# Attention with a stabilised softmax: row maxima moved by half batches of 16 heads, scores 19 fills ahead of the weights instead of 28

## What is computed

```python
q = (Q @ w_q.T).reshape(B, S, G, HG, HD)      # 8 groups of 4 heads, width 8; B = 4, S = 256
k = (K @ w_k.T).reshape(B, S, G, HD)
v = (V @ w_v.T).reshape(B, S, G, HD)
scores = jnp.einsum('bnghd,bmgd->bnghm', q, k) / scale
scores = jnp.where(pad, NEG_INF, scores)
scores = jnp.where(causal, scores, NEG_INF)
attn = jax.nn.softmax(scores, axis=-1)
out = jnp.einsum('bnghm,bmgd->bnghd', attn, v).reshape(B, S, D)
return out @ w_o.T + b_o
```

## Time and profile before

| | before |
|---|---|
| time, median of 3 runs | 359.84 us |
| profiled execution: time | 358.81 us |
| profiled execution: span | 357.1 us |
| busy: TensorE matmul / VectorE / ScalarE / POOL | 318.0 / 258.3 / 162.8 / 110.3 us |
| granted TensorE clock, mean over the span | 0.976 |
| first score, first weight, first matmul of the FFN | 139.60 / 163.76 / 275.10 us |
| granted clock from 150 to 320 us | 1.00 |

### The profile page before, as it was taken

The page is one execution under the profiler, slowest core; times in us unless marked ns, Lnnn a source line. Parts: engine busy times, 40 slices in busy tenths (PEclk is TensorE's granted clock), DMA queues, the critical chain, the costliest instruction groups (busy, mean ns, idle before and its releaser), DMA issues.

```text
span 357.1 us, 5054 instructions
## 1 busy us (share of the span) xinstructions
PE 318.0 (89%) x1630; PEld 218.0 (61%) x1639; DVE 258.3 (72%) x572; ACT 162.8 (46%) x333; POOL 110.3 (31%) x156
## 2 busy tenths in 40 slices
PE   2799886669999987999989999998979999999997
PEld 1385676547899634555544554563444886788885
DVE  4538895776677649989967996895672479999921
ACT  2333455344444222147767766775784344333000
POOL 7503575272000275501443425243554001000000
PEclk9999999658999999999999999999999999999999
DMA  6999200025311224600000000000000000000101
GB/s 190 369 418 323 51 1 16 2 88 180 101 61 59 76 59 130 284 0 9 0 7 2 1 0 9 0 3 1 6 3 0 0 2 0 2 0 0 46 30 44
DMA packets 14090, 22.96 MB, mean 64 GB/s; under 512 B 2065, under 2 KB 11409, under 8 KB 13202
## 3 DMA queue, kind: packets, MB, share of 16 engines
q1 hardware_dynamic: 13298, 20.56, 16.8%
q0 software_dynamic: 768, 2.10, 1.9%
HBM read 16.36 MB, written 6.03 MB: 63 GB/s over the span
## 4 chain that ended last, share of the span: by engine, by line
PE 61%; DVE 21%; issue 5%; ACT 4%; DMA 4%; POOL 4%; SPq 1%; DVEq 0%; ACTq 0%; POOLq 0%
PE bank L272 44%; DVE mx L1332 6%; PE bank L492 5%; PE bank L460 4%; ACT region L1008 3%; DVE stats L1078 2%; PE bank L463 2%; DMA region<-y_sorted,place 2%; PE bank L288 2%; POOL rstd L774 2%; DVE x_sb L1118 1%; DVE xn L1090 1%; PE bank L282 1%; PE bank L507 1%; POOL region L814 1%
## 5 line engine op out<-in xcount | busy, mean ns | idle before, releaser
L1008 ACT ACTIVATE region<-bank,padcol 128x512 f32<-128x512 f32 x96 | 62.3, 692 | 18.6 <-PE bank L272 17.8
L1332 DVE TENSOR_REDUCE mx<-bank 128x2 f32<-128x512 f32 (+1 forms) x96 | 60.9, 681 | 4.7 <-PE bank L463 4.1
L841 POOL TENSOR_SCALAR_AFFINE_SELECT region<-region 128x1024 f32<-128x1024 f32 x32 | 35.8, 1121 | 77.8 <-ACT region L1008 77.8
L272 PE MATMUL bank<-qst,kblk 128*128 128x512 f32 x96 | 45.7, 488 | 0.8 <-DMA qst<-nmT 0.3
L460 PE MATMUL bank<-kblk,qst 128*128 128x512 f32 x96 | 43.6, 471 | 1.7 <-DVE mx L1332 1.3
L463 PE MATMUL bank<-causb,identb 128*128 128x256 bf16 (+1 forms) x90 | 28.3, 314 | 0.0
L272 PE MATMUL bank<-e_down,region 128*128 128x256 f32 x128 | 28.0, 380 | 0.0
L1118 DVE SCALAR_TENSOR_TENSOR x_sb<-bank,tg,x_sb 128x256 f32<-128x256 f32 x24 | 11.6, 483 | 21.0 <-PE bank L272 21.0
L272 PEld LDWEIGHTS bank<-e_down,region 128*128 128x128 f32 x128 | 24.2, 190 | 3.6 <-DVE region L1481 0.3
L774 POOL TENSOR_TENSOR rstd<-veps,power 128x1 f32<-128x1 f32 x40 | 24.8, 619 | 3.3
L770 POOL TENSOR_SCALAR veps<-mv 128x1 f32<-128x1 f32 x40 | 12.8, 321 | 40.3 <-DVE mv L1080 37.5
(11 more groups left out here) (195 smaller groups left out, 737.0 us busy)
## 6 DMA issues: line engine op xcount, KB each, us to landing
e_gu<-in_e_gu_dram SPq DMA_DIRECT2D x2, 1408.0 KB, 12.2
x_sorted<-zero SPq DMA_DIRECT2D x1, 1920.0 KB, 9.4
y_sorted<-region SPq DMA_DIRECT2D x15, 128.0 KB, 1.7
x_sb<-in_x_dram SPq DMA_DIRECT2D x4, 256.0 KB, 4.1
ctxT<-in_ctxT_dram SPq DMA_DIRECT2D x2, 512.0 KB, 7.3
e_down<-in_e_down_dram SPq DMA_DIRECT2D x1, 1024.0 KB, 13.6
region<-x_sorted SPq DMA_DIRECT2D x1, 1024.0 KB, 7.4
e_gu<-in_f_gate_dram SPq DMA_DIRECT2D x1, 1024.0 KB, 6.5
```

What stands on the lines that cost most here:

```text
L272: return pe.matmul(dst, lhsT, rhs, start=first, stop=last)
L841: pool.affine_select(out=block, in_=block, compare_op=ALU.is_ge, fill=0.0, base=0, pattern=[[0, 2], [0, PER_GROUP], [1, P]], channel_multi ...
L1008: taken(act.activation(dst, src.rearrange("p (h n) -> p h n", n=SEQ - mt * P), ACT.Exp, bias=padcol[:, key:key + 1], scale=float(HD) ** -0 ...
L1332: taken(dve.reduce_max(mx[:, b % 2, nt, quads, q, hg], src, AX), "sa")
```

## The change

The maxima travel in halves of 16 heads: `negate`, `neg_turn` and the pair of transfers are done per half, after score fills 11 and 23, each with half of the columns; the second half's weights (fill 12) have a wait of their own. `nmx` and `nmT` have a slot per half instead of one per batch parity. Both transposes of a half go into one bank, with one wait and one copy. So scores need to be only 12 fills plus `LEAD` = 7 ahead of the weights, 19, where they ran 24 + 4 = 28 ahead (31 at the beginning). In the steps of a batch scores stand at steps 0 to 16; seven score fills of the next batch stand at the end of each, three before and four behind the last value product.

```diff
-LEAD = 4
-FIRST_LEAD = 7
+HALF_FILLS = 12
+LEAD = 7
-NEGATE_AT, FIRST_NEGATE_AT = 22, 18
+NEGATE_AT, FIRST_NEGATE_AT = (7, 19), 13
...
-            def neg_turn(b, kinds):
-                s = b % 2
+            def neg_turn(b, q):
+
+                half = 2 * b + q
+                dst = acquire(pe, "nmT", half, "turn1")
+                pe.wait_ge(sem("nm_made"), 2 * half + 2)
                 for nt in range(2):
-                    dst = acquire(pe, "nmT", 2 * b + nt, kinds[nt])
-                    pe.wait_ge(sem("nm_made"), 2 * b + nt + 1)
-                    ready(pe.transpose(dst[0:2 * HEADS, 0:P], nmx[:, s, nt, :].bitcast(F32), ident[:, :]), "nmT")
+                    ins = pe.transpose(dst[0:HEADS, tile_cols(nt)], nmx[:, q, nt, :].bitcast(F32), ident[:, :])
+                ready(ins, "nmT")
...
-                if n == 0:
-                    pe.wait_ge(sem("max_rows"), 16 * 2 * (b + 1))
+                if n % HALF_FILLS == 0:
+                    pe.wait_ge(sem("max_rows"), 16 * 2 * (2 * b + q + 1))
...
-            for n in range(24):
+            for n in range(HALF_FILLS + LEAD):
                 scores(0, n)
                 if n in (1, 3):
                     stack_piece(0, 2 + n // 2, "exp")
+                if n == FIRST_NEGATE_AT:
+                    neg_turn(0, 0)
                 queries(1, n)
-                if n >= 20:
-                    stack_piece(1, n - 20, "exp")
-            for n in range(FIRST_LEAD):
-                scores(1, n)
-                if n == 2:
-                    neg_turn(0, ("turn1", "tok1"))
+                if n >= HALF_FILLS + LEAD - 2:
+                    for piece in range(2):
+                        stack_piece(1, 2 * (n - HALF_FILLS - LEAD + 2) + piece, "exp")
             for b in range(BATCH):
-                lead = LEAD if b else FIRST_LEAD
                 for n in range(24):
-                    if b + 1 < BATCH and n + lead < 24:
-                        scores(b + 1, n + lead)
+                    ahead = 24 * b + n + HALF_FILLS + LEAD
+                    if n + LEAD < 24 and ahead < 24 * BATCH:
+                        scores(*divmod(ahead, 24))
                     weights(b, n)
...
-                    if n == (NEGATE_AT if b else FIRST_NEGATE_AT) and b + 1 < BATCH:
-                        neg_turn(b + 1, ("turn1", "turn1"))
+                    if n == NEGATE_AT[0]:
+                        neg_turn(b, 1)
+                    if n == NEGATE_AT[1] and b + 1 < BATCH:
+                        neg_turn(b + 1, 0)
...
                     for n in range(i * LEAD // 2, (i + 1) * LEAD // 2):
-                        if b + 2 < BATCH:
-                            scores(b + 2, n)
+                        if b + 1 < BATCH:
+                            scores(b + 1, HALF_FILLS + n)
...
-            for b in range(BATCH):
-                sp.wait_ge(sem("nmT_taken"), 2 * b + 2)
+            for half in range(BATCH * HALVES):
+                b, q = divmod(half, HALVES)
+                sp.wait_ge(sem("nmT_taken"), half + 1)
...
+            def row_maxima_at(at):
+
+                b, n = divmod(at, 24)
+                row_maxima(b, n)
+                if n % HALF_FILLS == HALF_FILLS - 1:
+                    negate(b, n // HALF_FILLS)
...
             for b in range(BATCH):
-                lead = LEAD if b else FIRST_LEAD
-                if b + 1 < BATCH:
-                    for n in range(lead):
-                        row_maxima(b + 1, n)
+                if b >= 1:
+                    for n in range(LEAD):
+                        row_maxima_at(24 * b + HALF_FILLS + n)
                 for n in range(24):
-                    if b + 1 < BATCH and n + lead < 24:
-                        row_maxima(b + 1, n + lead)
-                        if n + lead == 23:
-                            negate(b + 1)
+                    ahead = 24 * b + n + HALF_FILLS + LEAD
+                    if n + LEAD < 24 and ahead < 24 * BATCH:
+                        row_maxima_at(ahead)
```

More of the change, by code:

```diff
@@ L743, in _ @@
             load(sp, "f", f_down, a["f_down"])
-            for b in range(BATCH):
-                sp.wait_ge(sem("nmT_taken"), 2 * b + 2)
+            for half in range(BATCH * HALVES):
+                b, q = divmod(half, HALVES)
+                sp.wait_ge(sem("nmT_taken"), half + 1)
+                if half >= 1:
+                    sp.wait_ge(sem("max_rows"), 16 * 2 * half)
                 for piece in range(2):
-                    rows = slice(piece * HEADS, (piece + 1) * HEADS)
-                    dst = qst[24 + piece:P:32, b % 2, :, :, :]
-                    sp.dma_start(dst.rearrange("p q h n -> p (q h) n").bitcast(F32),
-                                 nmT[rows, b % 2, :].bitcast(F32))\
+                    rows = slice(piece * HEADS // 2, (piece + 1) * HEADS // 2)
+                    sp.dma_start(qst[24 + piece:P:32, b % 2, q, :, :].bitcast(F32), nmT[rows, q, :].bitcast(F32))\
                       .then_inc(sem("max_rows"), 16)
@@ L989, in _, with neg_turn @@
                 act.activation(s_high[0:EXPERT_R, 2 + i % 2, 1, :], src[0:EXPERT_R, P:2 * P], ACT.Copy).then_inc(sem("sa_high"), 1)
-            def neg_turn(b):
-                if b >= 2:
-                    act.wait_ge(sem("max_rows"), 16 * 2 * (b - 1))
-                for nt in range(2):
-                    src = filled(act, "nmT", 2 * b + nt)[0:2 * HEADS, 0:P]
-                    taken(act.activation(nmT[:, b % 2, tile_cols(nt)], src, ACT.Copy), "nmT")
+            def neg_turn(b, q):
+                half = 2 * b + q
+                if b >= 1:
+                    act.wait_ge(sem("max_rows"), 16 * 2 * (half - 1))
+                src = filled(act, "nmT", half)[0:HEADS, 0:SEQ]
+                taken(act.activation(nmT[:, q, :], src, ACT.Copy), "nmT")
             def exponentials(b, n):
@@ L1030, in _ @@
             query_stack(0)
-            for n in range(24):
+            for n in range(HALF_FILLS + LEAD):
+                if n == FIRST_NEGATE_AT:
+                    neg_turn(0, 0)
                 queries(1, n)
             query_stack(1)
-            neg_turn(0)
             for b in range(BATCH):
@@ L1043, in _ @@
                         ln_turn(3, NORM_STEPS.index(n))
-                    if n == (NEGATE_AT if b else FIRST_NEGATE_AT) and b + 1 < BATCH:
-                        neg_turn(b + 1)
+                    if n == NEGATE_AT[0]:
+                        neg_turn(b, 1)
+                    if n == NEGATE_AT[1] and b + 1 < BATCH:
+                        neg_turn(b + 1, 0)
                 if b + 2 < BATCH:
@@ L1332, in row_maxima, with negate @@
                 taken(dve.reduce_max(mx[:, b % 2, nt, quads, q, hg], src, AX), "sa")
[L1334 to L1346 removed]
+            def negate(b, q):
+                half = 2 * b + q
+                dve.wait_ge(sem("sa_taken"), 24 * b + HALF_FILLS * (q + 1))
+                if b >= 1:
+                    dve.wait_ge(sem("nmT_ready"), half - 1)
+                for nt in range(2):
+                    m = mx[:, b % 2, nt, :, q, :]
+                    high, low = (nmx[:, q, nt, c:c + HEADS // 2].rearrange("p (j h) -> p j h", j=QUADS) for c in (0, HEADS // 2))
+                    dve.tensor_scalar(high, m, -1.0, None, ALU.mult).then_inc(sem("nm_high"), 1)
+                    dve.wait_ge(sem("nm_high"), 2 * half + nt + 1)
+                    dve.scalar_tensor_tensor(out=low, in0=m, scalar=-1.0, in1=high.bitcast(F32), op0=ALU.mult,
+                                             op1=ALU.subtract).then_inc(sem("nm_made"), 1)
+            def row_maxima_at(at):
[3 more added lines that the diff above has]
+                    negate(b, n // HALF_FILLS)
             def norm_low(k):
```

20 lines of the change are left out of this document (5 added, 15 removed).

## The result

| | before | after |
|---|---|---|
| time, median (4 runs each, side by side) | 360.47 us | 370.06 us (369.41 to 371.03) |
| ratio, 95% interval | | 1.028 (1.025 to 1.031) |
| profiled execution: time / span | 358.81 / 357.1 us | 371.03 / 369.3 us |
| first score (s0) | 139.60 | 141.73 |
| s0 to the FFN's first matmul | 135.50 | 145.86 |

The changed kernel is slower by 2.8%: the direction was right, the size was not. The range ended at 369.5 and the forecast was 365.3: it had put the change at +5.5, and the medians differ by 9.6. The profiled executions differ by 12.2, for the one before is faster than its median and the one after slower.

A forecast was written before the change was run, and what follows sets the result against it. VectorE was taken to bound the prologue and batch 1's alternating steps, TensorE the batch ends. −4.5 + 2.8 + 2.4 + 4.8 = +5.5 on the profiled 358.81 gave 364.3, as a median 365.3 us; range 358.8 to 369.5.

The forecast's parts named there:

- A: Prologue and batch 0 up to weight fill 20 (w20): gain 4.5 us, bounds 3.3 to 5.7.
- B: Batch 1: loss of 2.8 us, the sum of seven numbered items.
- C: Batch 2: as B, with a larger item (5) and one more old wait gone; loss of 2.4 us.
- Item (4): Step 7, batches 1 and 2: transposes wait in bank 6 for VectorE's division, then VectorE idles for a score; 1.2 us.
- item (5): Chain from step 16's maximum to w20, now with no score beside its transposes: 0.6 us in batch 1, 1.1 in batch 2.
- items on bunching (1, 3, 5, 6): Batches 1 and 2: two more maxima (1.2), VectorE's gap (−0.46), longer chain to w20, third score between value products (0.4).
- item (3): Batch 1, up to step 16's maximum: VectorE's one gap takes up part of the added work; −0.46 us.
- two old waits: Batch 2: old transposes at step 22 with their wait go (−0.8 us), and the wait for the attention output (−0.9).
- D: Batch 3: 12 more maxima and a negation on VectorE, 7.8 us, less gaps of 2.84 and a little more; loss 4.8.
- Faster: Rival: TensorE, not VectorE, paces steps 0 to 16; −3.0 to −4.2 us, 355.6 to 356.8 us; chance 0.15.
- Worse: Rival: POOL's selects meet negations and batches 1 and 2 wait for the second transfer; +9.9, 369.7 us; 0.08 shared with another rival.
- Within 1%: Rival: item (4) does not show and batch 3 gives back half its loss; +0.7, 360.5 us; chance 0.27.

The follow-up runs named there:

- narrow runs: Three versions of the changed kernel, cutting down VectorE's maxima, TensorE's scores, or both, for batch 3's last 12 score fills: 368.59, 370.22 and 367.53 us.
- narrow maxima: Changed kernel with the maxima of batch 3's last 12 score fills reading 8 columns per head instead of 128 or 256: 368.59 us.
- one step less: Changed kernel with the transposes of the second half's maxima at step 8 instead of 7, still in bank 6: 369.74 us.
- the casts: Rounded parts of the FFN weight splits made by ScalarE instead of VectorE: 363.51 us in the changed kernel with bank 7 and early table load, 360.30 in the kernel before.
- bank 7: Changed kernel with the transposes of the row maxima in bank 7 instead of bank 6, which the heads' output transposes use: 365.26 us, ratio 1.0143.

## Why the prediction was right or wrong

**A, −3.4 instead of −4.5.** The mechanism held point by point. From s0, w0 comes at 158.5 on the clock of before (predicted 158.0), the first exponential at 160.6 (159.7), w3 at 161.3 (160.3), w20 at 177.3 (176.2). ScalarE's stack copies end at 159.2, not 158.4, and this delay runs on to w20; from w3 to w20 it takes the 16 us predicted. The value lies at the cautious bound (3.3). The step that failed here is the end of the stack copies, put 0.8 too early. The load was put rightly on the path, at its row's 1.29 and no more.

**B, +3.5 instead of +2.8, and C, +4.3 instead of +2.4.** Item (4), the wait in bank 6, was right in place and mechanism and too small in size. At step 7 it costs 1.3, predicted 1.2; but the transposes at step 19 use the same bank, and item (5) counted them as work only, not as a wait for a further division: 0.3 in batch 1 and 0.7 in batch 2. The items on bunching (1, 3, 5, 6) sum up to 1.7 in B and were 1.6, in part by luck: the gap of item (3), 0.46, did not close (0.28 in the kernel before with LEAD 7, 0.43 in the changed one). In C they were 2.2 and measured 0.5, but the two old waits that were to go there (−0.8 and −0.9) gave back nothing that shows: without bank and clock stage 2 is +0.7, where the items give 1.2. Why they did not stays open. What made C large is the granted clock, +1.5, on which the prediction had nothing. It read 1.00 for the whole stretch before and kept it, although the chain of item (5) leaves TensorE waiting in a row at steps 17 and 19. The sign for VectorE held: it shows no gap in steps 0 to 6 of batches 1 and 2. From w20 to w20 batch 1 takes 36.0 (179.40 to 215.39), not about 34.

**D, +5.9 instead of +4.8.** From the third split's second instruction to the last split it is 5.6 longer (257.80 to 269.25 after, 251.25 to 257.10 before), where the sum had 5.0: of the gaps that should have swallowed maxima 0.74 stayed (0.21 and 0.53). Bank 6 adds 0.7 here as well, which D had not priced. The sign "w12 waits for the transfer" came, with a wait of about 0.2: from the transposes to w12 it takes 3.35 (269.39 to 272.74), predicted 3.8, since the transfer takes 2.5, not 3.0, and the output projection ahead of w12 fills nearly all of it. And D was priced by VectorE's gaps alone. The narrow runs show TensorE holding it as well. The rival "Faster", which priced TensorE's 12 further scores at 1.5, would have failed at this even with VectorE relieved: with narrow maxima stage 3 is still 5.0 above the kernel before.

**At nothing and unknown.** Covered transfers at steps 8 to 12: right in batches 1 and 2, where w12 starts 3.85 and 3.18 behind the transfer's issue and 2.46 are needed (the issue to the waiting w12 at step 8). Batch 0 has 0.5 in hand and batch 3 nothing; one step less made w12 wait 0.87 and 0.27 there. POOL's hits on negations, taken at nothing: right in sum; the changed kernel has slow first or second instructions of 1.05, 0.79 and 0.42 us where before had 0.80, 0.47 and 0.79.

**The sum.** Three steps failed. Item (5) took the transposes at step 19 for work without a wait for bank 6, and D gave that wait no price; the granted clock was kept at 1.00; and A had the stack copies end too early. In order of size: the second place of the shared bank and its share in D, about 1.7 (0.3 + 0.7 + 0.7); the clock, 1.5; A, 1.1. These 4.3 are nearly the whole of 10.4 − 5.5; the smaller misses of both signs leave 0.6. The range had ends for each unknown price, but for none of these three.

**The rivals.** "Worse" came nearest in time (369.7), by another way: neither POOL nor transfers did it. "Within 1%" lived on delays that come to less than their sum; they came to more.

## What to carry to other kernels

When a step moves into a loop, list for each buffer that it takes who frees it, and price the wait at every place where it stands, not at the first; a buffer that is free at that time (here a bank) was worth more than the shorter prologue (4.8 against 3.4 us). A stretch where two engines have nearly the same load has to be relieved on both, so price a moved piece on each engine that issues or consumes it and take the larger. An engine's idle time may grow without a loss, and its work shrink without a gain (the casts); only the wait that ends last counts.

## What the runs showed of the hardware

The granted clock of TensorE fell to its 1.2 GHz level (0.50 from 250 to 251 us) inside a dense stretch, behind waits of 0.31, 0.78 and 0.56 us in a row that left TensorE busy for 3.35 of 5 us, and cost 1.5 us until it was back. It did so in some executions and not in others of nearly the same program. Eight matmuls without use in those waits cost nothing that shows (stage 2 at 31.42 against 31.40 and 31.41), and in their profile the clock stayed at 2.4 GHz there.

The Trainium skill, "Perfetto Trace Analysis", section "Matmuls", asks that independent groups of matmuls rotate through different banks of PSUM. The runs agree, with 4.8 us for two pairs of small transposes in each batch. The cost is not in the transposes, which take 0.38 us with bank 7 as well, but in the wait (1.13 us at step 7) by which they hold up the score behind them.
